# Moving a slice of probability-times-context matmuls later, and one PSUM eviction earlier, in a cross-attention kernel's hand-written order

## The reference

```
kvx = jnp.einsum('bsi,oi->bso', cond, w_kv_x)
kx, vx = jnp.split(kvx, 2, axis=-1)
kx = _ln(kx.reshape(b, sc, g, d), kxln_w, kxln_b)
vx = vx.reshape(b, sc, g, d)
xout = _gqa(qx, kx, vx).reshape(b, s, nh * d)   # softmax(q k / sqrt(d)) v
cat = jnp.concatenate([core, xout], axis=-1)
```

## Time and profile before

| what | value |
|---|---|
| time, median of 3 runs | 2840.67 us (2837.76 to 2842.53) |
| the profiled execution's own time | 2842.53 us |
| its span | 2840.6 us |
| PE busy over the span | 2234.2 us (79%) |
| DVE busy | 2086.6 us (73%) |
| ACT busy | 1261.8 us (44%) |
| POOL busy | 1369.1 us (48%) |
| TensorE clock granted, mean | 0.913 |

### The profile page before, as it was taken

How to read it: one execution, slowest core, us unless ns; L and a number is a source line. 1 busy time by engine, 2 the same in 40 slices (tenths; PEclk the granted TensorE clock), 3 DMA queues, 4 the chain that set the end, 5 groups by cost and what they waited for, 6 DMA issues and landing times. The chain is left out here.

```text
span 2840.6 us, 51489 instructions
## 1 busy us (share of the span) xinstructions
PE 2234.2 (79%) x17490; PEld 1692.5 (60%) x17490; DVE 2086.6 (73%) x4338; ACT 1261.8 (44%) x2258; POOL 1369.1 (48%) x773
## 2 busy tenths in 40 slices
PE   2465652799999899989989989989999984757665
PEld 0243342577777677767767767776777763544442
DVE  7888985678787677777767868777687773765765
ACT  4455452555555455545545545554555541011011
POOL 2465564557566466665656656656566551000000
PEclk9687776999999999999999999999999997878877
DMA  2000104345355364444544535444355345210100
GB/s 104 15 39 28 44 23 137 57 96 110 70 114 102 71 123 87 90 102 82 117 76 102 111 62 123 88 90 104 75 110 88 74 73 176 73 37 1 37 4 4
DMA packets 593332, 221.51 MB, mean 78 GB/s; under 512 B 546288, under 2 KB 580544, under 8 KB 591936
## 3 DMA queue, kind: packets, MB, share of 16 engines
q1 hardware_dynamic: 593088, 218.38, 35.2%
HBM read 64.18 MB, written 17.83 MB: 29 GB/s over the span
## 5 line engine op out<-in xcount | busy, mean ns | idle before, releaser
L71 PE MATMUL x_kc<-x_wk,x_ctxT 128*128 128x256 f16 x4992 | 626.1, 275 | 58.7 <-DMA x_ctxT<-x_ctxp 38.7
L71 PE MATMUL x_ox<-x_ctxp,x_pt 128*128 128x256 f16 x4992 | 619.6, 273 | 6.0 <-DMA x_pt<-x_ph 6.0
L71 PEld LDWEIGHTS x_kc<-x_wk,x_ctxT 128*128 128x128 f16 x4992 | 475.6, 98 | 137.4 <-ACT x_kraw L1056 43.8
L1056 ACT ACTIVATE x_kraw<-x_kc 128x512 f32<-128x512 f32 (+1 forms) x448 | 255.3, 570 | 612.2 <-PE x_kc L71 601.7
L1314 DVE SCALAR_TENSOR_TENSOR x_kT<-x_tp,x_hv,x_kT 128x512 f16<-128x512 f32 (+1 forms) x448 | 317.7, 709 | 273.6 <-ACT x_kT L1075 273.6
L71 PEld LDWEIGHTS x_ox<-x_ctxp,x_pt 128*128 128x128 f16 x4992 | 480.8, 98 | 59.9 <-issue 7.1
L990 POOL TENSOR_TENSOR x_kn<-x_kraw,x_rk 128x2304 f32<-128x2304 f32 x64 | 311.7, 4870 | 309.4 <-DVE x_rk L1297 309.4
L1005 POOL TENSOR_TENSOR x_ph<-x_pb,x_ph 128x1601 f16<-128x1601 f32 x128 | 415.0, 3242 | 23.8 <-POOL x_ph L1002 23.8
L1002 POOL TENSOR_SCALAR x_ph<-x_pb 128x1601 f16<-128x1601 f32 x128 | 196.4, 1534 | 411.0 <-ACT x_pb L1102 411.0
L1075 ACT ACTIVATE x_kT<-x_tp,x_hv 128x512 f16<-128x512 f32 (+1 forms) x448 | 292.8, 654 | 126.6 <-PE x_tp L1156 126.6
L71 PE MATMUL x_s<-x_kT,x_qs 128*128 128x512 f16 (+1 forms) x1536 | 301.2, 342 | 37.8 <-DVE x_kT L1314 17.2
(11 more groups left out here) (214 smaller groups left out, 2814.5 us busy)
## 6 DMA issues: line engine op xcount, KB each, us to landing
x_stage<-in_ctx SPq DMA_DIRECT2D x16, 896.0 KB, 5.8
x_stage<-in_ctx SPq DMA_DIRECT2D x16, 640.0 KB
scr_q<-a_qxT SPq DMA_DIRECT2D x8, 1024.0 KB, 3.9
x_qs<-scr_q SPq DMA_DIRECT2D x16, 512.0 KB, 4.8
scr_core<-a_catc SPq DMA_DIRECT2D x8, 512.0 KB, 2.6
x_pt<-x_ph SPq DMA_TRANSPOSE x256, 3.8
scr_x<-x_catx SPq DMA_DIRECT2D x8, 512.0 KB, 3.3
f_cat<-scr_core SPq DMA_DIRECT2D x8, 512.0 KB, 5.6
```

The costliest lines, as they stand in the source:

```text
L71: last = pe.matmul(out, lhs[i], rhs[j], start=start and n == 0, stop=stop and n == len(parts) - 1)
L1056: act.activation(kraw[:, 4 * i:4 * i + n // P, :].rearrange("p n d -> p (n d)"), kc[:, 0:n], ACT.Copy).then_inc(kraw_ready, 1)
```

## The change

Two things are moved, nothing is added or taken away.

- PE: ("oa", -1) goes behind ("m", 3). ("pv", 0, 0) goes from between ("m", 4) and ("tr", 3) to behind ("m", 6). ("pv", 0, 1) and ("pv", 0, 2) each go one place back as well: behind ("tr", 5), and behind ("tr", 6).
- ACT: ("raw", 4) goes from behind ("oa", -1) to directly behind ("exp", 1), ahead of ("tr", 2) and ("oa", -1).

`DVE_ORDER`, the order of the `tp` users among themselves, the POOL list and the DMA list stay as they are.

```
-                 ("sc", 1), ("pv", -1, 2), ("pv", -1, 3), ("m", 2), ("tr", 1), ("oa", -1), ("m", 3), ("tr", 2), ("m", 4),
-                 ("pv", 0, 0), ("tr", 3), ("m", 5), ("ob", -1), ("tr", 4), ("m", 6), ("pv", 0, 1), ("tr", 5), ("pv", 0, 2),
-                 ("tr", 6), ("qb",), ("pv", 0, 3)]
+                 ("sc", 1), ("pv", -1, 2), ("pv", -1, 3), ("m", 2), ("tr", 1), ("m", 3), ("oa", -1), ("tr", 2), ("m", 4),
+                 ("tr", 3), ("m", 5), ("ob", -1), ("tr", 4), ("m", 6), ("pv", 0, 0), ("tr", 5), ("pv", 0, 1), ("tr", 6),
+                 ("pv", 0, 2), ("qb",), ("pv", 0, 3)]
         ACT_ORDER = [("raw", 0), ("sq", 0), ("oa", -2), ("exp", 0), ("tr", 0), ("raw", 1), ("sq", 1), ("raw", 2), ("tr", 1),
-                     ("raw", 3), ("exp", 1), ("tr", 2), ("oa", -1), ("raw", 4), ("sq", 2), ("tr", 3), ("sq", 3),
+                     ("raw", 3), ("exp", 1), ("raw", 4), ("tr", 2), ("oa", -1), ("sq", 2), ("tr", 3), ("sq", 3),
```

## The result

The changed kernel took 2930.5 us (median of 4 runs, 2922.6 to 2937.4), against 2841.6 us for the kernel before. The ratio is 1.0314, with a 95% interval of 1.0284 to 1.0343: 89 us or 3.1% slower. The forecast was 2920 us.

What follows compares the result with a forecast made beforehand. PE bounds the kernel, its list with the waits setting each step. Profiled 2842.5 us, plus 29 for the order and 50 for clock falls, makes 2921.5; the runs' median lies 1.9 lower, so 2920, range 2862 to 2970.

Steps and rivals of the forecast that it cites:

- The bound and the middle of the step: PE's list with its waits sets the step; ("tr", 3) waits through ACT's queue; shifts of +1.20 us per batch.
- The forecast 8.19: Middle of the step: ("tr", 3) starts 8.19 us behind ("m", 2), against 7.86 before in the step shown.
- The shifts of the four kinds of step: Later starts of ("tr", 3) in one batch: +0.33, +0.58, -0.04 and +0.33, together +1.20 us.
- the earlier copy gives nothing back: ACT's earlier ("raw", 4) gains nothing, as ("m", 5), which waits for it, stands behind ("tr", 3) on PE anyway.
- The end of the step: Behind ("tr", 6): a 1.32 us slice partly fills waits; carried 0, 0, 0.5 and 0.2, so 0.7 us per batch.
- The clock: PE's 2.4 us gap ahead of ("tr", 3) sometimes halves the granted clock: 31 x 1.6 = 50 us, bounds 0 and 99.
- every second one: Clock falls behind the gap ahead of ("tr", 3) taken in every second step, 31 times, between never and each step.
- That the clock stays: Rival: ("tr", 3) comes later but PE's clock doesn't fall in the gap; 2870 us, chance 0.27.
- That the delay is swallowed: Rival: DVE's and POOL's chain sets the pace, so the shifts only use up slack; 2841 us, chance 0.09.
- The case "faster": Rival: ACT's copy costs nothing, ("tr", 3) comes 7.6 us behind ("m", 2) everywhere; -7 us, 2834 us, chance 0.09.

Runs made afterwards that it cites:

- the filled-gap run: The changed kernel with 20 matmuls that nobody reads added behind ("m", 4) on PE, in the idle gap ahead of ("tr", 3): 2865.5 us, ratio 1.0072.

## Why the prediction was right

**The bound and the middle of the step: shown.** PE's list with the waits in it sets the step, and ACT's queue sets ("tr", 3). The forecast 8.19 was measured as 8.20, and the pieces separate: with the new PE order alone it is 7.61 (the steps of the prediction without the copy give 4.16 + 1.57 + 1.87 = 7.60), with the ACT order 0.59 more. The shifts of the four kinds of step add up to 4 x 8.20 - (7.61 + 8.23 + 7.85 + 7.85) = +1.26; the prediction had +1.20. That the earlier copy gives nothing back is shown by the ACT order alone, which is 0.8% slower.

**The end of the step: right but for one kind.** From ("tr", 3) to the next ("m", 2) the filled-gap run, in which the clock stays up, shows 0 where a batch ends (forecast 0), +0.51 in the ordinary step (0.5) and +0.15 in the remaining one (0.2). In the step with the quantisation it shows -0.58 where the prediction carried 0. There the median of line 1379 (1382 in that run) fell from 1.91 to 1.32 us. The later ("tr", 3) lets it start later, when POOL's subtraction is nearly over; it took 1.32 also with the ACT order alone, where ("tr", 3) is late, and 1.92 with the PE order alone, where it is not. I had taken all work behind ("tr", 3) as unchanged. A batch costs 1.36 us in place of 1.9, and the order by itself some 21 us where the sum had 29.

**The clock: the mechanism shown, its size too small, and its frequency a guess.** The 2.4 us gap came out as 2.38, the cost of a fall as 1.52 (1.6 taken), the number of falls in the middle of a step as 38 of 60 (every second one taken): 38 x 1.52 = 58 us where the sum had 50. "Every second one" was the middle between never and always, with nothing to choose it by, so its nearness is luck. The filler removed 68 us. Some 10 us of it are therefore not in these falls. The two profiled executions show where: in the changed kernel PE stands still for 21.4 us at five turns of the loop, in the filled-gap run for 16.3:

```profile
PE x_s L71 <- issue: 16.3, 5, 3.6
```

The first step starts 3.7 us later, and from the start of the last full step to the end it is 558.2 us in place of 554.0, of which 1.5 is one more fall. Whether the gap causes these or they vary from one program to the next is open; before, the turns had 16.9. The steady clock is 0.95; the prediction had 0.94.

So two terms were off, in opposite directions: the order came out 8 us under its term, the clock 18 us over it. That 2920 lies so near to 2930.5 is partly luck.

**The rivals.** That the clock stays (2870) is what the filled gap gives, 2865.5; the rule of the Trainium skill ("TensorE: Matmul & The Clock Gate", "HAM oscillation — how this bites in real kernels") that would have led there names a longer gap as the danger, and the measurement decides: here 32 of 61 gaps of 2.06 us were followed by a fall. No fall at 1.79 us is in agreement with it. That the delay is swallowed fell with the filled gap and with the ACT order alone: with the clock up, each is still 0.7 to 0.8% slower than before. The case "faster" fell at the point it named: ACT's ("tr", 2) starts 1394.43 - 1388.08 = 6.35 and not under 5.8 behind ("m", 2). Its own idea, that without the copy ahead ("tr", 3) comes at 7.6 everywhere, is what ("oa", -1) moved alone does, 2826 us.

**Where the gain of the change went.** The late slices do cover the waits at the end; that part and the move of ("oa", -1) together are worth 0.44 us in a batch and don't show in the time, as the turns of the loop took 6 us more. But moving the slices costs 0.68 of the 1.12 that ("oa", -1) gives (113.66 against 112.98), and it lays PE's gap bare, which is harmless at 1.79 us and not at 2.38. The copy made the difference between the two.

## What to carry to other kernels

A wait of the bounding engine that doesn't lengthen the step can still be paid for in TensorE's clock: compare the length of each idle gap, not the sum of the waits, before and after a change of order. When an operation is put earlier in an engine's queue, follow what is queued behind it up to the engine that sets the pace. Test a suspected clock cost by filling the gap with matmuls that nobody reads; if the kernel gets faster with more work, it was most likely the clock; compare the granted clock of the two runs.

## What the hardware showed unexpectedly

- In this step the falls of the clock set in within a narrow range of gap length: 0 of 61 gaps at 1.79 us, 32 of 61 at 2.06, 38 of 60 at 2.38. Length alone doesn't decide: among gaps of the same length some were followed by a fall and some not, and elsewhere in the trace of the kernel before a fall followed a gap of 1.86 and none followed the stretch with 3.07 us of idle time.
- Line 1379, which on DVE reads two float32 tiles in SBUF, took 1.3, 1.9 or 3.2 us, the more the longer it overlapped with POOL's subtraction of float32 tiles (line 1005), and ended 1.08 us behind it wherever it began at least 0.2 us before that one's end. The Trainium skill ("GPSIMD Engine Reference", "1. Specifications") says that GpSimd shares its SBUF interfaces with VectorE and that DVE instructions with two SBUF inputs contend for them. The trace agrees with that. DVE's low half of the keys (line 1314), which reads PSUM and SBUF, took the same 0.75 us beside the same POOL operation.
